# A mixer with causal linear attention and routed experts: key-value state as 64x64 blocks, logits in products of their own, elu + 1 by ScalarE and GpSimd, in five stages

## What is computed

```python
q  = einsum('nchw,oc->nohw', ln_c(x), Wq) + bq
kv = einsum('nchw,oc->nohw', ln_c(x), Wkv) + bkv
Q, K = elu(q) + 1, elu(k) + 1                     # 8 heads of 16
S_t = S_(t-1) + k_t v_t^T ;  num_t = q_t S_t       # causal, per head
den = 1 / (sum(Q * cumsum(K)) + 1e-10)            # the cumsum here runs over the heads
x = x + num * den
t = ln(tokens(x));  logits = t @ gate + router
top 2 of softmax(logits) -> combine
x = x + sum_e combine_e * (gam_e * (t @ expert_e + b_e) + bet_e)
```

## Time and profile before

| | us |
|---|---|
| median of 3 runs | 755.08 (754.40 to 756.46) |
| the profiled execution | 755.91 |
| its span in the profile | 754.1 |
| TensorE busy | 717.1 |
| VectorE busy | 685.9 |
| ScalarE, GpSimd busy | 409.9, 397.8 |
| first full step, step 36, begin at | 68.78, 666.09 |

### The profile page before, as it was taken

How to read it: one execution, slowest core, us unless ns; L and a number is a source line. 1 busy time by engine, 2 the same in 40 slices (tenths; PEclk the granted TensorE clock), 3 DMA queues, 4 the chain that set the end, 5 groups by cost and what they waited for, 6 DMA issues and landing times.

```text
span 754.1 us, 23195 instructions
## 1 busy us (share of the span) xinstructions
PE 717.1 (95%) x8137; PEld 624.0 (83%) x8137; DVE 685.9 (91%) x2550; ACT 409.9 (54%) x1261; POOL 397.8 (53%) x639
## 2 busy tenths in 40 slices
PE   4767999999999999999999999999999999999986
PEld 2666888888888888888888888888888888888875
DVE  4567999999999999999999999999999999999984
ACT  1122666655555666666665555555555555555544
POOL 5145555555555555555555555555555555555520
PEclk9769999999999999999999999999999999999999
DMA  5101111111111111111111111111111111111101
GB/s 129 33 15 30 42 40 35 37 40 37 39 37 42 42 42 42 42 42 42 42 42 42 42 42 42 42 42 42 42 42 42 42 42 42 42 30 29 30 16 29
DMA packets 60214, 30.29 MB, mean 40 GB/s; under 512 B 2160, under 2 KB 60176, under 8 KB 60176
## 3 DMA queue, kind: packets, MB, share of 16 engines
q1 hardware_dynamic: 60176, 29.79, 14.4%
HBM read 20.34 MB, written 9.44 MB: 39 GB/s over the span
## 4 chain that ended last, share of the span: by engine, by line
PE 91%; DVE 4%; POOL 2%; ACT 1%; issue 1%; DMA 1%; SPq 0%; DVEq 0%; ACTq 0%; POOLq 0%
PE bank L877 11%; PE bank L915 10%; PE bank L894 9%; PE bank L916 9%; PE bank L917 9%; PE bank L933 8%; PE bank L901 4%; PE bank L909 4%; PE bank L884 4%; PE bank L853 3%; PE bank L854 3%; PE bank L855 3%; PE bank L860 3%; PE bank L847 2%; PE bank L866 2%; PE bank L935 2%
## 5 line engine op out<-in xcount | busy, mean ns | idle before, releaser
L574 DVE TENSOR_TENSOR probs<-bank,tri 128x512 f32<-128x512 f32 x288 | 184.9, 684 | 10.2 <-PE bank L877 4.7
L397 ACT ACTIVATE y_act<-bank,scale 128x128 f32<-128x128 f32 x576 | 159.4, 383 | 2.5
L915 PE MATMUL bank<-e_high,x_high 128*128 128x512 f32 x288 | 124.0, 431 | 1.1 <-DVE o L803 1.1
L916 PE MATMUL bank<-e_low,x_high 128*128 128x512 f32 x288 | 113.7, 395 | 0.0
L917 PE MATMUL bank<-e_high,x_low 128*128 128x512 f32 x288 | 113.5, 394 | 0.0
L311 POOL TENSOR_TENSOR qn<-feat,rden 128x512 f32<-128x512 f32 x36 | 38.2, 1061 | 116.4 <-DVE rden L672 116.4
L416 ACT ACTIVATE x_high<-x 128x512 fp32r<-128x512 f32 x36 | 22.8, 633 | 137.0 <-DVE x L664 137.0
L592 DVE SCALAR_TENSOR_TENSOR y_dve<-bank,scale,y_dve 128x128 f32<-128x128 f32 x288 | 92.4, 343 | 0.0
L580 DVE SCALAR_TENSOR_TENSOR qkv<-bank,rstd,b_qkv 128x384 f32<-128x384 f32 x144 | 86.8, 605 | 5.1 <-POOL rstd L301 2.6
L387 ACT ACTIVATE k_odd<-bank,parity 128x512 f32<-128x512 f32 x36 | 24.7, 687 | 114.4 <-PE bank L860 114.4
L933 PE MATMUL bank<-ident,y_act 128*128 128x128 f32 x576 | 80.8, 273 | 1.6 <-ACT y_act L397 1.6
(11 more groups left out here) (139 smaller groups left out, 1764.5 us busy)
## 6 DMA issues: line engine op xcount, KB each, us to landing
x<-in_x SPq DMA_DIRECT2D x36, 256.0 KB, 3.3
x_res<-in_x SPq DMA_DIRECT2D x36, 256.0 KB, 3.2
out<-o SPq DMA_DIRECT2D x36, 256.0 KB, 2.4
beta_raw<-in_L_ffn_beta_w SPq DMA_DIRECT2D x1, 512.0 KB
e_raw<-in_L_ffn_expert_w SPq DMA_DIRECT2D x1, 512.0 KB
w_raw<-in_L_conv_Wkv SPq DMA_DIRECT2D x2, 64.0 KB, 2.4
b_qkv<-in_L_conv_bkv SPq DMA_DIRECT2D x1, 128.0 KB, 4.4
w_raw<-in_L_conv_Wq SPq DMA_DIRECT2D x1, 64.0 KB, 2.6
```

The costliest lines, as they stand in the source:

```text
L397: last = nc.scalar.activation(y_act[:, p, u, e], bank[EXPERTS_AT[u][0]][:, 128 * e:128 * e + 128], ACT.Copy, scale=scale[:, p, u, e:e + 1])
L574: return tt(probs[:, half, i].rearrange("p u e t -> p (u e) t"), bank[SCORES_AT[half][i]][:].rearrange("p (n t) -> p n t", t=T), tri[:].un ...
L915: mm(out, x1_high[:, p, u], e_high[:, w], start=True, stop=False)
L916: mm(out, x1_high[:, p, u], e_low[:, w], start=False, stop=False)
```

## The change

Five things change.

1. The key-value state is kept as two blocks of 64x64 (four heads each) in place of 128x128: `key_values` and `from_state` become two products for each image, on halves of the array; kv_new and state have half the columns.
2. `turn_x1` becomes four plain transposes, and the logits four products of 8 columns in another bank (`logits`); lg_raw is then one copy.
3. elu + 1 is made as relu(z - 1) + exp(-relu(1 - z)): three ScalarE passes (`shortfalls`, `exponentials`, `positives`) and an addition on POOL; `features` leaves DVE.
4. There are five stages (LAGS = 5). Projections 0 and 3 are in g[0], 1 and 2 in g[1]; features of images 2 and 3 in g[1], those of 0 and 1, the keys, the queries and kv in g[2]; both halves of the scores, x1 and the logits in g[3]; the experts in g[4].
5. All orders, needs and banks are written anew, and `turn_y` interleaves the transposes of two images.

```diff
-LAGS = 6
+LAGS = 5
-SCORES_AT = ((3, 7, 2, 0), (0, 5, 6, 7))
+SCORES_AT = ((4, 1, 5, 7), (4, 6, 2, 3))
...
-        kv_new = sb("kv_new", [128, U, 128])
-        state = sb("state", [128, IMAGES, 128])
+        pair_mask = sb("pair_mask", [128, 64])
+        kv_new = sb("kv_new", [128, U, 64])
+        state = sb("state", [128, IMAGES, 64])
...
+            def features(p, h):
+
+                return tt(feat[:, p, 2 * h:2 * h + 2], ex[:, 2 * h:2 * h + 2], qkv[:, p, 2 * h:2 * h + 2, 0:256], ALU.add)
...
-            def exponentials(p, h):
-
-                return nc.scalar.activation(ex[:, 2 * h:2 * h + 2], qkv[:, p, 2 * h:2 * h + 2, 0:256], ACT.Exp, bias=-1.0)
+            def shortfalls(p, h):
+
+                return nc.scalar.activation(ex[:, 2 * h:2 * h + 2], qkv[:, p, 2 * h:2 * h + 2, 0:256], ACT.Relu,
+                                            bias=1.0, scale=-1.0)
+
+            def positives(p, h):
+
+                z = qkv[:, p, 2 * h:2 * h + 2, 0:256]
+                return nc.scalar.activation(z, z, ACT.Relu, bias=-1.0)
+
+            def exponentials(h):
+
+                return nc.scalar.activation(ex[:, 2 * h:2 * h + 2], ex[:, 2 * h:2 * h + 2], ACT.Exp, scale=-1.0)
...
-            def features(p, h):
-
-                return stt(feat[:, p, 2 * h:2 * h + 2], ex[:, 2 * h:2 * h + 2], 1.0,
-                           qkv[:, p, 2 * h:2 * h + 2, 0:256], ALU.min, ALU.max)
...
-            def from_state(p):
-
-                for u in range(U):
-                    last = mm(bank[AT["att"]][:, T * u:T * u + T], state[:, U * p + u], q_t[:, p, u],
-                              start=(u == 0), stop=False, skip_group_check=True)
-                return last
...
+            def from_state(p):
+
+                for u in range(U):
+                    for i in range(2):
+                        rows = slice(64 * i, 64 * i + 64)
+                        last = mm(bank[AT["att"]][rows, T * u:T * u + T], state[rows, U * p + u], q_t[rows, p, u],
+                                  start=(u == 0), stop=False, skip_group_check=True)
+                return last
...
-                    last = mm(bank[AT["kv"]][:, 128 * u:128 * u + 128], feat[:, p, u, 128:256], qkv[:, p, u, 256:384],
+                    for i in range(2):
+                        last = mm(bank[AT["kv"]][64 * i:64 * i + 64, 64 * u:64 * u + 64],
+                                  feat[:, p, u, 128 + 64 * i:128 + 64 * i + 64],
+                                  qkv[:, p, u, 256 + 64 * i:256 + 64 * i + 64], start=True, stop=True)
+                return last
+
+
+            def turn_x1(p):
+
+                for u in range(U):
+                    last = transpose(bank[AT["x1_a"]][:, T * u:T * u + T], x1[:, p, u], ident[:])
+                return last
+
+            def logits(p):
+
+                for u in range(U):
+                    last = mm(bank[AT["x1_b"]][:, EXPERTS * u:EXPERTS * u + EXPERTS], x1[:, p, u], id_gate[:, T:WIDE],
                               start=True, stop=True)
                 return last
```

More of the change, by code:

```diff
@@ L927, in bias, with turn_y @@
                 return mm(bank[AT["out"]][:], e_bias3[:], coef_t[:, p], start=True, stop=False, skip_group_check=True)
[L929 to L936 removed]
+            def turn_y(p, half):
+                for e in range(5):
+                    for u in (2 * half, 2 * half + 1):
+                        last = mm(bank[AT["out"]][:, T * u:T * u + T], y_act[:, p, u, e] if e < 4 else y_dve[:, p, u],
+                                  ident[:], start=False, stop=(e == 4), is_transpose=True, skip_group_check=True)
+                return last
             def step(k, g):
@@ L943, in step @@
                     pe.wait_ge(S["rest_dve"], REST_DVE)
+                if g[3]:
+                    n, p = g[3].i, g[3].par
+                    need(pe, "qkv_0", n + 3)
+                    need(pe, "qkv_3", n + 3)
+                    need(pe, "k_even", n + 1)
+                    need(pe, "k_odd", n + 1)
+                    need(pe, "q_t", n + 1)
+                    if k is not None:
+                        need(pe, "y_act_1", n - 1)
+                        need(pe, "y_act_3", n - 1)
+                        need(pe, "qkv_1", n + 2)
+                    scores(p, 0).then_inc(S["scores_0"], 1)
+                    if k is not None:
+                        need(pe, "x1_parts", n)
+                    from_state(p).then_inc(S["from_state"], 1)
+                    need(pe, "probs_00", n + 1)
+                    need(pe, "out", n - 1)
+                    if k is not None:
+                        need(pe, "x_parts", n + 3)
+                        need(pe, "qkv_0", n + 3)
+                        need(pe, "probs_11", n)
+                        need(pe, "probs_12", n)
+                    scores(p, 1).then_inc(S["scores_1"], 1)
@@ L953, in step @@
-                    scores(p, 0).then_inc(S["scores_0"], 1)
+                        need(pe, "y_one_0", n)
+                        need(pe, "y_dve_02", n)
+                    experts(p, 1, 1).then_inc(S["experts_11"], 1)
+                if g[1]:
+                    n, p = g[1].i, g[1].par
+                    need(pe, "probs_02", n - 1)
+                    if k is not None:
+                        need(pe, "qkv_3", n + 1)
+                    project(p, 2).then_inc(S["proj_2"], 1)
+                    need(pe, "probs_03", n - 1)
+                    if k is not None:
+                        need(pe, "qkv_1", n)
+                    project(p, 1).then_inc(S["proj_1"], 1)
@@ new lines, in step @@
+                    need(pe, "kv_new", n + 2)
+                    if k is not None:
+                        need(pe, "probs_10", n + 1)
+                        need(pe, "qkv_0", n + 3)
+                    logits(p).then_inc(S["logits"], 1)
+                if g[4]:
+                    n, p = g[4].i, g[4].par
+                    need(pe, "probs_12", n + 2)
+                    if k is not None:
+                        need(pe, "y_one_2", n)
+                        need(pe, "y_dve_22", n)
+                    experts(p, 2, 1).then_inc(S["experts_21"], 1)
+                    need(pe, "qkv_1", n + 4)
+                    if k is not None:
+                        need(pe, "probs_03", n + 2)
+                        need(pe, "y_one_3", n)
+                        need(pe, "y_dve_32", n)
+                    experts(p, 3, 1).then_inc(S["experts_31"], 1)
@@ new lines, in step @@
+                if g[2]:
+                    n, p = g[2].i, g[2].par
+                    need(pe, "x_parts", n + 3)
+                    if k is not None:
+                        need(pe, "y_act_0", n - 1)
+                    turn_k(p).then_inc(S["k_turned"], 1)
+                if g[4]:
+                    n, p = g[4].i, g[4].par
+                    need(pe, "probs_11", n + 2)
+                    need(pe, "coef_t", n + 1)
+                    if k is not None:
+                        need(pe, "out", n)
+                    bias(p).then_inc(S["bias"], 1)
+                    if k is not None:
+                        need(pe, "x1_parts", n + 2)
+                    experts(p, 2, 0).then_inc(S["experts_20"], 1)
@@ new lines, in step @@
+                if g[0]:
+                    n, p = g[0].i, g[0].par
+                    need(pe, "x_low", n + 1)
+                    need(pe, "y_act_1", n - 3)
+                    if k is not None:
+                        need(pe, "lg_raw_a", n - 2)
+                        need(pe, "kv_new", n - 1)
+                        need(pe, "qkv_0", n)
+                    project(p, 0).then_inc(S["proj_0"], 1)
+                    need(pe, "y_act_3", n - 3)
+                    if k is not None:
+                        need(pe, "qkv_2", n)
+                    project(p, 3).then_inc(S["proj_3"], 1)
```

776 lines of the change are left out of this document (345 added, 431 removed), and 13 rows, old and new, of the table names.

## The result

The changed kernel takes 761.32 us (median of 8 runs, 758.83 to 765.09), the kernel before 755.03 on the same chip (median of 8, 754.09 to 757.15). The ratio is 1.0081, with a 95% interval of 1.0060 to 1.0101: slower by 0.8%. The execution profiled has a span of 759.4 us; I had worked out 753.2.

A forecast was written before the change was run, and what follows sets the result against it. TensorE was taken to bound the kernel: first full step at 62.8, plus 1.5, 32 x 19.48 (623.4) and 65.5 at the end give a span of 753.2 us, forecast as 754, range 732 to 775.

The forecast's parts named there:

- The full step's sum: TensorE's instructions in a full step: 19.22 - 0.39 + 0.46 + 0.19 = 19.48 us.
- (a): key_values on TensorE: 16 instructions of 64 columns, paired on column halves, in place of 8 whole ones, -0.39 us a step.
- (b): from_state on TensorE: 64-row products on diagonal blocks run abreast, 0 change a step.
- (c): Second turn of x1 and logits: transposes 0.44 plus 8-column products 0.93, against 0.93 before, +0.46 us a step.
- (d): Changes of tiling on TensorE: seven in a step in place of six, 0.19 each, +0.19 us.
- VectorE, ScalarE, GpSimd: The other engines in a full step: no wait for TensorE, but four margins of half a microsecond.
- rival E: A new wait, one of four margins gone: 0.3 to 1.0 in a step, 765 to 790 us; chance 0.14.
- The ends: Time outside full steps: first full step at 62.8 us, last four steps 65.5 against 88.0, giving 9.2 back.
- B: Cheap logits, weights loaded behind the streaming: 24 us less, 730, or half of it, 742; chance 0.14.
- C: Column halves of key_values not abreast: +0.39 x 36 = 14 us, 768; chance 0.10.
- D: from_state's two 64-row tiles on one bank run one after the other: 32 us, 786; chance 0.08.
- F: Shorter pipeline does not shorten: first full step at 68 or later, last ones wait more, 760 us.

The follow-up runs named there:

- e5: Kernel of e1 with the state's eight 64-row products replaced by four whole 128x128 products with constant weights, in the same place: 760.84 us, ratio 1.0066.
- e9: Kernel of e1 with the sixteen 64x64 key-value products replaced by four whole 128x128 products in the same place: 769.09 us, ratio 1.0174.
- e1: Changed kernel with one VectorE instruction moved, the mask of the best expert now behind the last weighted sum of image 3: 759.66 us, ratio 1.0046.
- e2: Changed kernel with GpSimd's second feature addition (128x512) issued as two of 128x256: 759.16 us, ratio 1.0044.
- e8: Kernel before with only elu + 1 changed to three ScalarE passes and a GpSimd addition for each half: 804.12 us, ratio 1.0640.
- e12: Kernel of e1 with the features back on VectorE and one ScalarE exponential for each half: 873.37 us, ratio 1.1563.
- e10: Kernel of e1 with twelve projection matmuls, results unread, added in steps 36 and 37: 759.31 us, ratio 1.0052.
- e7: Kernel of e1 with only the first 32 tokens of each image as weights of the logit products: 746.00 us (one run).
- e6: Kernel of e1 with the 64-wide state and key-value products issued all of one half, then all of the other: 783.67 us, ratio 1.0355.
- e11: Kernel of e1 with the logits' operands swapped, the router's 8 columns as weights and 128 tokens moving: 767.56 us (one run).
- e3: Changed kernel with the second turn of x1 and the logits joined again as one 136-column product: 745.66 us, ratio 0.9857.

## Why the prediction came out as it did

The forecast was 754, in a range of 732 to 775; 761.3 is inside, and inside the likeliest case's own 745 to 762. But the sign is wrong: level was forecast, slower by 0.8% came. The picture of a TensorE-bound step was right in the main: TensorE's instructions are all of a short step but 0.20. The sum missed 6.2 us of span, 2.8 in the full steps and 3.4 at the end; the other 0.9 is that the execution read after lies at its median, and not 0.8 above it as the one of before.

**The full step's sum** (19.48, measured 19.47 to 19.49 where the mask is not held) is right as a total and wrong in its terms. From start to start of the matmuls:

| term | forecast | measured |
|---|---|---|
| (a) key_values | -0.39 | -0.27 (0.89 to 0.62) |
| (b) from_state | 0 | +0.21 (0.81 to 1.02) |
| (c) turn and logits | +0.46 | +0.41 (0.84 to 0.44 + 0.81) |
| (d) changes of tiling | +0.19 | not seen as a term; with all the rest of the step -0.28 |
| wait ahead of project 0 | none | +0.20 |

(a) and (b) are mis-sized. That a change between two kinds of tiles is paid inside these pieces would fit, but no run separates it from the pace of the 64-wide tiles. (d) is mis-sized because I counted seven changes at one price. e5 and e9 show the count that fits: a block that stands between whole tiles pays 0.1 to enter and 0.1 to leave. Before, three blocks did; after there are two, since the state's tiles stand between the scores, and the key-value tiles ahead of the values. That is 0.2 less, most of the -0.28. The seven changes are real, but two fewer of them border on whole tiles. That these errors and a wait that I had at nothing cancelled to 0.01 is luck.

**VectorE, ScalarE, GpSimd** is the step that failed. "So no wait, but four margins of half a microsecond": three of the margins held. The fourth, at project 0, was gone in every step. I had the evictions end at 15.0 and TensorE there at 15.4. They end at 15.50 behind the first scores, TensorE is there at 15.52, and project 0 starts at 15.65, since the matmul starts 0.15 behind the last eviction, a time that I had left out. With the matmul behind it that is 0.20 a step, by an estimate 7 us over 36 steps.

The second wait came at a fifth place, from a cause that I had not weighed. I took VectorE's durations from rows of before and walked GpSimd's new additions beside them as if the two engines were apart. e1 and e2 show that they aren't: an instruction of VectorE with both inputs in SBUF stands still until the GpSimd instruction in flight ends. Both waits are rival E in kind, in size smaller (0.20 in each step, and 0.17 in every second one, where I had 0.3 to 1.0 in each). Only the second shows in the 2.8 us that the full steps missed, since the first is hidden behind the mis-sized terms.

"That is worth nothing where TensorE has no gap" was true for the change as made, in that TensorE's sum sets the step. As a statement on the third part it is too simple: e8 and e12 cost 48 and 114 us. Each undoes or makes one part in an order fitted to the other, so these are prices of the misfit together with the part, and no run here tells the part's own worth. What they show is that the order on VectorE and GpSimd decides, on engines that seem to have room.

**The ends.** The start was right: 44.96 for step 3 (44.6), 62.72 for the first full one (62.8), 21.02 for that one (20.98). At the end I took steps 36 and 37 "by TensorE's sum", 17.9 and 16.9. They took 18.85 and 18.93. With the projections gone TensorE comes to the transposes before ScalarE has evicted (e10). I had used the bound of the other engines for steps 38 and 39 only; those came out at 31.2 for 30.7. This is the larger of the two errors that the span shows.

**The rivals.** B (cheap logits) was wrong: 0.81, and e7 shows the weights behind it. The Trainium skill, TensorE: Matmul & The Clock Gate, has both sides: its Back-to-back issue gap alone spoke for B, its LDWEIGHTS against; e7 and e11 are with the second. C and D fall by e6, D as priced: from_state takes 1.02, under its mark of 1.1. F did not come: the shorter pipeline gave what it was to give at the start.

**The chances.** Slower had 0.43, the largest of the three, while the likeliest case lay 0.1% on the faster side. The case's own distribution leaned below its centre (0.22 below, 0.13 above), though every unknown left out of it, a wait or a hold, could only lengthen the step.

## What to carry to other kernels

Before work is moved from one engine to another, list which instructions of a neighbour engine the moved ones can hold, and what stands behind the held one in its queue; a busy share of 62% says nothing on this. Take the time from an instruction's end to the start of the one that waits for it out of the rows (0.14 to 0.15 in a full step here) before calling what is left a margin. A part of a change that costs can hide behind parts that pay: price each alone, here 0.41 a step for splitting a product whose weights are loaded twice, and leave it out (e3, 745.66 us). When matmuls leave a step, its length does not fall by their sum but to the longest of what they covered.

## What was not expected of the hardware

- GpSimd's instruction in flight holds a VectorE instruction with two SBUF inputs to its end: 0.18 becomes 1.18 behind 128x512 and 0.63 behind 128x256 (e2). Where the VectorE instruction comes first it keeps 0.18, and GpSimd's addition takes 1.37 in place of 1.27. The weighted sums, with one input in PSUM, keep 0.34 beside the same additions.
- A busy TensorE can hide waits: the window shows 50.00 of 50.00 busy both with (after) and without (e1) the 0.17 in every second step, and the 0.20 ahead of project 0 is in both. Starts of matmuls show it, busy time doesn't.
- Two 64-row tiles that write different partitions of one bank cost less as neighbours than in turn: 1.02 together, 1.51 in turn, 0.89 + 0.20 as whole products in the same place.
- For a product with 8 moving columns the weights decide: 0.10 with 128 weight columns, about 0.04 with 32, and 0.12 with 8 weight columns and 128 moving.
- A wait of 1 to 2 us in each step can cost more than itself: in e12 the clock fell to the lower level behind it, and the next matmuls took 0.43 in place of 0.23.
